# Four stacked graph layers on one core: ScalarE's loop of copies cut from 128 steps a round to 64

## What is computed

```python
h = relu(layernorm(x));  x = x + attention_mean(h, edge_index, edge_attr_16, ...)    # layer 0
h = relu(layernorm(x));  x = x + graph_conv(h, edge_index, ...)                      # layer 1
h = relu(layernorm(x));  x = x + two_weighted_means(h, edge_index, edge_weight, ...) # layer 2, two passes
h = relu(layernorm(x));  x = x + gat(h, edge_index, edge_weight, ...)                # layer 3, softmax per dst

# what the layers 0 to 2 share: sums over edges
agg = segment_sum(x[src] * weight_of_edge, dst, num_segments=n)
```

## Time and profile before

| | us |
|---|---|
| median of 3 runs | 7470.36 (7467.83 to 7475.19) |
| the profiled execution | 7471.27 |
| its span (first to last instruction) | 7469.4 |
| preparation, by the engines' windows | 149 |
| build | 2631 |
| dense products of layers 0 to 2 | 2482 |
| softmax layer | 2207 |

### The profile page before, as it was taken

One profiled execution on the slowest core, in us unless ns is written; L12 is line 12 of the kernel. 1 busy time (PEld: TensorE's weight loads), 2 busy tenths in 40 slices (PEclk: granted clock), 3 DMA queues, 4 the chain that ended last, 5 costly groups with the idle time before them and its releaser, 6 DMA issues.

```text
span 7469.4 us, 164666 instructions
## 1 busy us (share of the span) xinstructions
PE 5787.7 (77%) x48472; PEld 4908.7 (66%) x48472; DVE 3874.9 (52%) x9331; ACT 2401.8 (32%) x7251; POOL 1834.4 (25%) x1782
## 2 busy tenths in 40 slices
PE   1777777777777779999999999999256666665665
PEld 1555555555555559999999999998244444444444
DVE  6899999999999992222111111112144444444444
ACT  2666666666666661111110000001112222222222
POOL 2000000000000000000000000000677777777771
PEclk9998988989889899999999999999577777777786
DMA  6766766667666678666667766674222222222221
GB/s 195 283 276 274 287 276 282 281 274 286 275 278 281 278 292 281 259 258 271 275 276 279 279 276 273 278 281 182 44 59 59 60 61 59 60 60 60 59 60 32
DMA packets 261005, 1542.55 MB, mean 207 GB/s; under 512 B 56235, under 2 KB 86965, under 8 KB 233836
## 3 DMA queue, kind: packets, MB, share of 16 engines
q1 hardware_dynamic: 201380, 1406.77, 48.0%
q0 software_dynamic: 59008, 129.85, 7.2%
q10 hardware_dynamic: 130, 0.80, 0.0%
HBM read 795.75 MB, written 743.08 MB: 206 GB/s over the span
## 4 chain that ended last, share of the span: by engine, by line
PE 47%; DVE 19%; POOL 13%; issue 12%; ACT 3%; ACTq 3%; DMA 2%; DVEq 0%; SPq 0%; POOLq 0%
PE psum L1113 29%; POOL field L808 12%; DVE field L1544 12%; PE psum L1078 8%; PE psum L1302 3%; PE psum L1280 3%; ACT field L921 2%; ACTq L906 2%; DVE field L1537 1%; ACT field L1009 1%; DVE field L1538 1%; DVE field L1539 1%; PE psum L1179 1%; ACTq L921 1%; DMA field<-head_table,cmp 1%
## 5 line engine op out<-in xcount | busy, mean ns | idle before, releaser
L1113 PE MATMUL psum<-field 128*128 128x128 f32 x19208 | 2255.4, 277 | 25.9 <-issue 18.8
L1113 PEld LDWEIGHTS psum<-field 128*128 128x128 f32 x19208 | 2232.5, 189 | 26.6 <-issue 19.0
L1078 PE MATMUL psum<-field 128*128 128x200 bf16 (+1 forms) x14112 | 1924.3, 281 | 132.7 <-DVE field L1544 115.6
L921 ACT COPY field<-psum x4704 | 1657.8, 416 | 959.2 <-PE psum L1078 664.4
L1544 DVE TENSOR_TENSOR field<-field 128x1176 bf16<-128x1176 bf16 x2352 | 1649.2, 761 | 0.0
L808 POOL DMA_INDIRECT field<-head_table,cmp x1563 | 1505.3, 963 | 476.3 <-issue 469.3
L1078 PEld LDWEIGHTS psum<-field 128*128 128x128 bf16 x14112 | 1077.6, 101 | 425.8 <-issue 159.0
L1069 PE MATMUL psum<-zero_b 128*128 128x2 bf16 x4704 | 807.7, 172 | 456.7 <-ACT field L921 447.9
L1069 PEld LDWEIGHTS psum<-zero_b 128*128 128x128 bf16 x4704 | 478.2, 102 | 643.5 <-issue 578.9
L752 POOL DMA_INDIRECT field<-tile_rows,step_t_i x74 | 201.0, 2716 | 2403.0 <-PE psum L1049 2355.9
L1009 ACT COPY field<-psum x1611 | 432.0, 268 | 1050.9 <-PE psum L1302 746.1
(11 more groups left out here) (288 smaller groups left out, 2572.6 us busy)
## 6 DMA issues: line engine op xcount, KB each, us to landing
adj<-field SPq DMA_DIRECT2D x882, 800.0 KB, 5.1
field<-adj SPq DMA_DIRECT2D x196, 3200.0 KB, 10.0
field<-head_table,cmp POOLq DMA_INDIRECT x1563
field<-in_edge_attr SPq DMA_DIRECT2D x4, 3072.0 KB, 25.5
head_table<-field SPq DMA_DIRECT2D x7, 476.0 KB, 3.3
tile_rows<-field SPq DMA_DIRECT2D x1, 3328.0 KB, 18.2
right_edges<-zeros SPq DMA_DIRECT2D x1, 3328.0 KB, 19.7
place_rows<-right_edges SPq DMA_DIRECT2D x25, 128.0 KB, 2.8
```

The lines of the kernel that those rows point to most:

```text
L921: act.copy(evac[:, :, bass.ds(place, SEG)], build_banks[:, bass.ds(bank, NSEG * SEG)].rearrange("p (w c) -> p w c", w=NSEG)).then_inc(pair ...
L1078: mm = pe.matmul(build_banks[:, bass.ds(cur[j % ROUND], end - first)], hot, pr[:, first:end], start=False, stop=True, skip_group_check=True)
L1113: mm = pe.matmul(ps_y[slot][:, 0:D], source[:, hi, :], adj_in[slot][:, :, 2 * hi:2 * hi + 2], start=(hi == 0), stop=(hi == NB - 1))
```

## The change

ACT's loop body covers one chunk of 64 steps instead of two. It runs 73 rounds (`LOOPS * PER_LOOP + 1`), and its tail is 32 steps instead of 96. DVE, PE and SP keep their loops of 128 steps. Since the chunk number `c` is now a register inside the loop, the slot `c % 2` is computed at run time: the row of words is addressed by it (`rows_of`), and so is the table to which `take_tab` writes, for which the two tables are carved out of one piece with a leading index. The memory that they take is the same. Waits count by `c * CHUNK` in place of `k * PER_LOOP * CHUNK`.

```diff
@@ build, the pieces of the arena
-        step_tab = [piece(TAB_FIELDS * CHUNK // 2).bitcast(BF16).rearrange("p (k s) -> p k s", k=TAB_FIELDS) for _ in range(2)]
+        step_tabs = piece(TAB_FIELDS * CHUNK).bitcast(BF16).rearrange("p (i k s) -> p i k s", i=2, k=TAB_FIELDS)
+        step_tab = [step_tabs[:, i, :, :] for i in range(2)]
@@ the scalar engine
-            def take_tab(c, slot):
+            def parity(c):
+                return nc.s_assert_within(c % 2, 0, 1, skip_runtime_bounds_check_because="a chunk's parity")
+
+            def take_tab(c):
                 act.wait_ge(step_rows_turned, c + 1)
-                act.copy(step_tab[slot][:, VALUES - 2:, :], ps_tab).then_inc(step_tab_ready, 1)
+                tab = step_tab[c] if isinstance(c, int) else step_tabs[:, bass.ds(parity(c), 1), :, :].rearrange("p i k s -> p (i k) s")
+                act.copy(tab[:, VALUES - 2:, :], ps_tab).then_inc(step_tab_ready, 1)
-            def copy_pairs(k, n):
+            def copy_pairs(c, n):
+                act.wait_ge(bank_rows_loaded, c * 16 + 16)
+                act.sem_inc(chunk_open, 1)
+                rows_of = bank_rows[0:1, c % 2, :, :, :] if isinstance(c, int) else \
+                    bank_rows[0:1, bass.ds(parity(c), 1), :, :, :].rearrange("p a q k e -> p (a q) k e")
                 for j in range(n):
-                    slot, at = j // CHUNK, j % CHUNK
-                    if at == 0:
-                        act.wait_ge(bank_rows_loaded, k * (16 * PER_LOOP) + 16 * (slot + 1))
-                        act.sem_inc(chunk_open, 1)
...
-                            bank_rows[0:1, slot, q, R_COPY, :], engines=ACT_ONLY, min_val=0,
+                            rows_of[0:1, j // ROUND, R_COPY, :], engines=ACT_ONLY, min_val=0,
...
-                        act.wait_ge(step_added, k * (PER_LOOP * CHUNK) + (j + 1 + ADDED0))
-                        act.wait_ge(pair_copied, k * (PER_LOOP * CHUNK) + (j - 2 + COPIED0))
+                        act.wait_ge(step_added, c * CHUNK + (j + 1 + ADDED0))
+                        act.wait_ge(pair_copied, c * CHUNK + (j - 2 + COPIED0))
...
-                    if at == CHUNK * 3 // 4 and not (isinstance(k, int) and slot == 1):
-                        take_tab(k * PER_LOOP + slot + 1, (slot + 1) % 2)
-            take_tab(0, 0)
+                    if j == CHUNK * 3 // 4 and n == CHUNK:
+                        take_tab(c + 1)
+            take_tab(0)
             act.wait_ge(banks_cleared, 1)
-            with act.Fori(0, LOOPS) as k:
-                copy_pairs(k, PER_LOOP * CHUNK)
-            copy_pairs(LOOPS, TAIL_STEPS)
+            with act.Fori(0, LOOPS * PER_LOOP + 1) as c:
+                copy_pairs(c, CHUNK)
+            copy_pairs(LOOPS * PER_LOOP + 1, TAIL_STEPS - CHUNK)
```

More of the change, by code:

```diff
@@ L903, in copy_pairs @@
                     half = j // ROUND % 2
                     if j % ROUND == 0:
-                        q = at // ROUND
                         _, word = nc.values_load_multi_w_load_instructions(
-                            bank_rows[0:1, slot, q, R_COPY, :], engines=ACT_ONLY, min_val=0,
+                            rows_of[0:1, j // ROUND, R_COPY, :], engines=ACT_ONLY, min_val=0,
                             max_val=(EVAC_SLOTS - 1) * SEG * WORD + (BUILD_BANKS - 1) * BANK,
                             skip_runtime_bounds_check_because="a word is a place below EVAC_SLOTS and a bank by construction")
-                        act.wait_ge(pairs_stored[half], k * (16 * NSEG * PER_LOOP * CHUNK // ROUND // 2)
-                                    + 16 * NSEG * (j // ROUND // 2 + 1))
+                        act.wait_ge(pairs_stored[half], c * (16 * NSEG * CHUNK // ROUND // 2) + 16 * NSEG * (j // ROUND // 2 + 1))
```

## The result

| us | before | after |
|---|---|---|
| median | 7469.72 (7467.83 to 7475.19, 4 runs) | 7300.9 (7299.45 to 7304.09, 4 runs) |
| profiled execution, its span | 7471.27, 7469.4 | 7304.09, 7302.2 |
| first batch of the build to the last, on DVE | 148.5 to 2772.0: 2623.5 | 151.6 to 2604.6: 2453.0 |
| last batch to the span's end | 4697.4 | 4697.6 |

The changed kernel takes 0.9773 of the time before (95%: 0.9756 to 0.979), 2.3% less. The forecast was 7317 us. All of the gain lies in the build: 170.5 us less from its first to its last batch. It begins 3.1 us later (over all the runs here the first batch starts between 147.2 and 152.3 us, whatever ACT's loop), and behind it the time is the same to 0.2 us, so the span is 167.2 us shorter.

What follows compares the result with a forecast made beforehand. The prediction took DVE to pace the build, held up through PE by ACT's code-loading stall at each branch back. Removing 35 stalls saved 153.5 us, other terms 0, giving 7317 us for the median; range 7250 to 7402.

Steps and rivals of the forecast that it cites:

- Rival D: Whole kernel: no change, the time goes back to another wait or a late dense stage; 7470 us, chance 0.03.
- The body stays: ACT's build loop: the new 208-row body stays on chip between rounds, so 35 branch stalls go; chance 0.84.
- rival B: ACT's build loop: the short body is thrown out too, so each of 72 branches stalls; 7629 us, chance 0.08.
- 4.39 us a round: Build: first chunk of a round shortens to the second's length; times 35 rounds, 153.5 us off.
- the full case at 7250: Build: PE's clock no longer falls at chunk starts, two chunks take DVE's own 65.4 us; saves 220 us.
- The stall costs more than its length on PE: Build, round start: granted clock drops to 0.50 from 510.4 to 520.4 us; DVE's 4.70 us hold both.
- The costs put at 0: Build: added branches and address instructions, denser stores and the shorter tail, each costed at 0 us.
- hit branch: ACT's build loop: 37 more branches back, between nothing and 0.5 us each, covered by ACT's own wait; costed at 0.
- the two delays: ACT's branch back: one delay before the first instruction, and one of 2.4 us inside the first load of words.
- The fused instructions for the addresses: ACT's build loop: added ahead of loads, copies and the table's copy, hidden under copies or without a DVE wait; 0.
- SP's denser stores: Build: stores come 6% more densely, DMA share 0.69 becomes about 0.73; costed at 0.
- Rival C: ACT's build loop: branch hits but the first load still takes 3.46 us; 7403 to 7490 us, chance 0.05.

Runs made afterwards that it cites:

- e2: Changed kernel with one unused semaphore increment behind each copy in ACT's loop, body 278 instructions; 7666.0 us.
- e4: Changed kernel with two unused increments behind each loop copy and 30 ahead of the loop to shift the 342-instruction body; 7313.73 us, 0.9794 of before.
- e1: Kernel before, its two-chunk ACT body kept, with row of words and table addressed by a parity register and a 96-step tail; 7469.07 us, 1.0001 of before.
- e5: Kernel before with 22 unused increments ahead of ACT's loop, its 415-instruction body touching four blocks instead of five; 9095.84 us, beside 9070.77 for before.
- e3: Changed kernel with two unused semaphore increments behind each copy in ACT's loop, body 342 instructions; 7726.84 us, 1.0342 of before.
- e6: Kernel before with 44 matmuls of zeros per round on PE ahead of its wait for ACT; 9013.82 us, 0.9933 of before.
- e10: Changed kernel with 8 matmuls of zeros on PE behind a chunk's last step and 6 in its first; 8884.5 us, 0.976 of before.
- e9: Changed kernel unaltered, measured again beside its version with zeros on PE; 8914.1 us, 0.9795 of before.

## Why the prediction was right

- **Where the gain would be.** In the build alone, as said: 170.5 us, and nothing given back in the later stages. Rival D is out.
- **The body stays.** True, and e2 shows what lay on the other side. The reasoning was incomplete, though: it went by length and called 208 rows "nearest to 201". By length 278 instructions (e2) would have looked safer than 342 (e4), and it was the other way about. What decides is the number of blocks touched, with the one behind them, and so also where the loop happens to begin. The prediction said so only in rival B's condition. That "208 is nearest to 201" gave the right answer was in part luck: the same reasoning would have kept 278, which do not stay. The changed body of 214 instructions touches three blocks where it begins (20 + 128 + 66). A body of that length touches at most three wherever it lies, and so was safe; this could have been said beforehand from the fetch's size, had the number of blocks held been known.
- **What the Trainium skill says of it.** The trace has fetches of 8 KB, and e1 to e5 fit four blocks of that size. The Trainium skill, "Runtime: NRT & Kernel Launch", section "Instruction fetch mechanics", speaks of two blocks of 16 KiB, the next one fetched in sequence, and of a stall where a taken branch leads outside them. Four times 8 KB is the same sum; the size of a block is not, and the measurement decides. The stall at a branch whose target is gone agrees: ACT is idle 6.1 to 7.0 us there in before, e2 and e3.
- **The mis-sized term: 4.39 us a round.** It was 4.88 (71.7 - 2 x 33.41). Times 35 that is 170.8 for 153.5. The sum took the second half of a round for every chunk to come. But that half had the clock's fall in all 35 rounds of before. After the change 20 of 69 chunks have none and take 32.94 us, and the other 49 take 33.58, a little under 33.65. Why the second halves of before all had it is not shown; in e5, where the loop only begins elsewhere, 9 of 35 have none. The prediction named this as its doubt and put the full case at 7250; the truth lay between, at 7300.9. The 3.1 us by which the build begins later are in no term; they took back part of the difference.
- **The stall and the clock.** "The stall costs more than its length on PE, since the granted clock drops" holds, but the weight was left open. By e6 the clock was worth 1.2 of the first half's 38.04 us. The larger part is PE's wait itself. One reading of the prediction needs putting right: PE "stood idle behind ACT just before the longer fall", but not in the stall. PE's timeline of before, one round ahead of the earlier trace rows:

```profile
437.25 0.17 PE L1069 MATMUL psum<-zero_b 128*128 128x2 bf16 x1 [1.50 <-ACT field L921]
...
438.80 0.75 PE L1078 MATMUL psum<-field 128*128 128x300 bf16 x3
443.12 0.18 PE L1069 MATMUL psum<-zero_b 128*128 128x2 bf16 x1 [3.57 <-ACT field L921]
```

  The granted clock falls to 0.50 at 438.5 us, behind a short idle of 1.50 us and ahead of the 3.57 us that come from the stall. The stall does not start the fall; it goes with a longer one, 10.2 us for 3.4.
- **The costs put at 0.** The hit branch shows as a record of 45 ns and a gap of 0.18 us behind it; before, where the target had to be fetched, that gap was 2.37 us (medians). With the first load's 2.4 us these are the two delays that the prediction named. The hit branch is covered: ACT's idle at a chunk's start ends with PE's matmul, at 2.43 us for 2.27. The fused instructions for the addresses cost nothing, by e1. SP's denser stores neither: the DMA share is 0.74 as against about 0.73 forecast, and nobody waits for it.
- **Rival C.** No load of words takes over 1.03 us in the middle of the build. The 3.46 us came with the fetch, not with the branch.
- **What would show it.** The build's window was to be 2478 us and is 2463; chunks near 33.65 came out as 33.58 with the fall and 32.94 without.

## What to carry to other kernels

A hardware loop whose branch back is followed by several microseconds of "issue", with fetches on the instruction queue in its steady state, is too long for its engine. Here the body and the block behind it had to fit in four blocks of 128 instructions, so count the blocks that the body touches where it lies, not only its length, and recount after each edit ahead of the loop. If an engine off the critical path stalls like this, price it on the engine that sets the pace, and look at the TensorE clock in the microseconds after the stall: a part of the price lies there (here 1.2 us of a first half's 38.04).

## What the runs showed of the hardware

- **Alignment of a loop is worth 413 us.** The same body of 342 instructions takes 7726.84 us at one place in the program and 7313.73 at another (e3, e4).
- **All or nothing.** A body one block too long is not fetched in part. All its blocks and the next are, on each pass (5 for 4 blocks touched, 6 for 5), and in the kernel before the idle at the branch is the same 6.2 us in the mean for either (217.1 and 218.5 us over 35).
- **Zeros keep TensorE's clock.** With 14 matmuls of zeros around a gap of some 2 us the granted clock stays at 1.00, 2.4 GHz (e10). Without them it fell to 0.50, 1.2 GHz, at 47 of 69 chunk starts in e9, which cost such a chunk 0.65 us (33.59 for 32.94).
- **One build, two times behind it.** e9 is the changed kernel, and its build takes 2449.9 us where the first run's takes 2453.0. Behind the build it is 6305.9 and 4697.6 us. The dense stage is no slower, against what e9's expectation says: the granted clock is 1.00 from 2800 to 5000 us in both. The difference lies in the softmax layer, where waits of ACT of up to 24 us stand against an event that the profile calls remote. Their cause was not studied.
